# A graph layer with residual and normalisation: near sums kept by feature, gathers paced by TensorE, two rows to a statistic

## The chip, the cores and the metric

One core of one Trainium2 chip. The metric is the device time of one execution in microseconds; lower is better. Times before: 690.98, 693.69 and 698.72 us in three runs, median 693.69 us.

## The reference, cut to what matters

100,000 nodes and 25,000 edges, 128 features, all in fp32. The edges are sorted by `dst`, and `dst` is 100000·u² for a uniform u, so low nodes have many edges and high ones few.

```python
src, tgt = x[row], x[col]                     # 25,000 gathered rows each
h   = relu(concat([src, tgt, edge_attr]) @ W1 + b1)      # 384 -> 128
msg = h @ W2 + b2
w   = sigmoid(concat([msg, conf]) @ Wa + ba)
out = segment_sum(msg * w, col, num_segments=100000)
y   = layernorm(x + out)                      # over the 128 features, eps 1e-5
```

Every node's row is read, normalised and written, also those without an edge.

## The kernel before, in words

**Two ways for edges.** The first 64 tiles of 128 edges (16 groups of `G` = 4 tiles, "near") end at nodes below 91·128 = 11,648. Their sums are gathered in the tile `near`, which holds the x rows of all 91 blocks of 128 nodes. The other 33 groups ("list") lie as runs of 44 edges on each partition; VectorE folds each run edge by edge into `acc`, adds the gathered destination row (`rows_dst`), and the result (`stash`) is normalised and scattered to `out` by an indirect transfer. All nodes from 11,648 on are also read in 63 chunks of 11 rows a partition (`nodes`, six slots), normalised as they are, and written; the scatters come later over those rows.

**Steps.** `STEPS` (line 50) orders the 49 groups, k = 0 to 48: list groups, with a near group after every two, the near groups from high nodes to low. In step k TensorE does `hidden(k)`, the sums of step k-1, `turn(k+1)` (transposes of the gathered rows, their edge attributes, and for near groups a matmul of loaded x rows with the one-hot `pick` in place of a gather) and `messages(k)`. ScalarE copies the turned rows out of PSUM, applies relu, the gate and most of the normalisation. VectorE adds the bias (`raw`, `logit`), folds or adds sums, computes row statistics with `bn_stats`, and normalises the rest. A statistics batch b has three chunks, the list groups of its two steps and, for the nine batches of `NEAR_OUT`, some near blocks; `scales` (L1137) turns its statistics into scale and shift with 13 small instructions and two last ones.

**Near sums.** For each of four tiles of a near group TensorE multiplies the one-hot `place` (edges by nodes, `KA` blocks wide) with `gated` block by block (L921): 192 block matmuls in all, each two passes (the ×384 of a profile). The result has nodes on partitions, and VectorE adds it to a window of `near` that starts at a whole block (L1313, two PSUM banks in turn). The block numbers are read from `block_row` by one load each (L1302). Statistics of near rows are taken directly (L1212).

**GpSimd's queue** is written out in lines 668 to 689: for k = 2 to 48 gather the source rows (four indirect transfers of 128 rows, L641), for list groups also the destination rows (L652), then the scatters that `SCATTERS` names for that k (L662, four transfers a group; 44 transfers stand last, after the gather of k = 48). A gather waits until TensorE has taken the source rows of step k-4 (`RING` = 4, L637). In every second group `pause` (L624) makes GpSimd wait until the group before has landed.

**SyncE's queue** (L552 to L577) issues in each step the attributes, near tables and x rows, chunk loads and chunk stores, each behind its own wait.

Of the kernel before, what the change touches and what calls it, by code (L numbers as in the profile page):

```python
# [8 lines left out]
I32 = mybir.dt.int32  # L9
AX_X = mybir.AxisListType.X  # L10

P = 128
# [3 lines left out]
RING = 4  # L16
SLOTS = 6
PAUSE = 2
TRIO = 3
ROWS = 11  # L20
STATS = 6
# [19 lines left out]
KA = (1, 2, 2, 2, 2, 3, 3, 3, 3, 3, 4, 4, 4, 4, 4, 4)  # L41
LOW = 48
# [22 lines left out]
NEAR_OUT = {4: (77, 91), 5: (70, 77), 13: (59, 70), 14: (48, 59), 15: (37, 48), 19: (26, 37),  # L65
            20: (14, 26), 23: (4, 14), 25: (0, 4)}
NEAR_BATCHES = tuple(sorted(NEAR_OUT))
BATCHES = 26
# [8 lines left out]
SSTEPS = 13  # L77
# [20 lines left out]
def half_of(n, widths):  # L98

    return 8 * (n % 2) if widths[DG - 1 - n] <= 2 else 0  # L100


def before_in_buffer(n, widths):

    alone = n == 0 or widths[DG - 1 - n] > 2 or widths[DG - n] > 2
    return n if alone else n - 1

def sum_uses():  # L110
    uses = []
    for k in range(K + 1):
# [4 lines left out]
        for l in range(LISTS):  # L117
            if k == TAIL_STEP.get(l):
                uses.append(("tail", l))
            if k == HEAD_STEP[l]:  # L120
                uses.append(("head", l))
    return {u: i for i, u in enumerate(uses)}
# [4 lines left out]
EXTRAS = [u for u in USES if u[0] != D_]  # L127
# [6 lines left out]

def columns(b):

    at, n = {}, 0
    if 3 * b < 63:
        at["nodes"] = n
        n += TRIO * ROWS  # L140
# [3 lines left out]
    if b in NEAR_OUT:  # L144
        at["near"] = n
        n += NEAR_OUT[b][1] - NEAR_OUT[b][0]
# [8 lines left out]
NEAR_IN = {0: (76, 91), 1: (62, 76), 2: (48, 62), 6: (32, 48), 8: (16, 32), 10: (0, 16)}  # L155
NEAR_PIECES = 3
ADDED_BEFORE = {4: 2, 5: 2, 13: 6, 14: 6, 15: 6, 19: 10, 20: 10, 23: 13, 25: 16}
# [10 lines left out]
def build(nc, x, src, dstw, attr, conf, W1, b1, W2, b2, Wa, ba, out):  # L168
# [9 lines left out]
    with ExitStack() as ctx:  # L178
# [36 lines left out]
        v_match = sb("v_match", [1, P])  # L215
        base_row = sb("base_row", [1, DT], I32)
        block_row = sb("block_row", [1, DT + 1], I32)
# [13 lines left out]
        raw = sb("raw", [P, 2, G, F])  # L231
# [6 lines left out]
        near = sb("near", [P, NB, F])  # L238
        nodes = sb("nodes", [P, SLOTS, ROWS, F])
        stats = sb("stats", [P, 2, WIDEST, STATS])  # L240
        sc_calc = sb("sc_calc", [P, 5, WIDEST])
        sc = sb("sc", [P, 2, 2, WIDEST])


# [23 lines left out]
        limit = at(4080, 4 * (DT + 1)).rearrange("p (k t) -> p k t", k=4)  # L268
        calc = at(4352, 6 * (DT + 1)).rearrange("p (k t) -> p k t", k=6)
        whole = at(4864, DT + 1, I32)  # L270
# [3 lines left out]
        v_off = at(5400, 4)  # L274
# [27 lines left out]
        g_stats = at(2440, STATS)  # L302
        g_calc = at(2450, 5).rearrange("p (k u) -> p k u", u=1)
# [48 lines left out]
        near_landed = sems("near_landed", 2)  # L352
# [22 lines left out]
        act_normed = sems("act_normed", SLOTS)  # L375
        dve_normed = sems("dve_normed", SLOTS)
        near_act_normed = sem("near_act_normed")
        near_dve_normed = sem("near_dve_normed")
# [6 lines left out]
        v_added = sem("v_added")  # L385

# [28 lines left out]
        def wait(eng, semaphore, value):  # L415
            if value > 0:
                eng.wait_ge(semaphore, value)

# [37 lines left out]
        def _(sp):  # L456
# [49 lines left out]
            def load_near_x(n):  # L506
                g = DG - 1 - n
                at_ = half_of(n, KG)
                done = before_in_buffer(n, KG)
# [4 lines left out]
                for j in range(G):  # L514
                    base = sp.value_load(base_row[0:1, g * G + j:g * G + j + 1], min_val=0, max_val=N - 4 * P)
# [4 lines left out]
            def store_nodes(c):  # L520
                u, nth = c % SLOTS, c // SLOTS + 1
                n = chunk_parts(c)
                sp.wait_ge(act_normed[u], nth)
                sp.wait_ge(dve_normed[u], nth)
# [6 lines left out]
            def store_near(b):  # L531
                q = NEAR_BATCHES.index(b)
                low, high = NEAR_OUT[b]
                sp.wait_ge(near_act_normed, q + 1)
                sp.wait_ge(near_dve_normed, q + 1)
                sp.dma_start(blocks_of(out, low, high), near[:, low:high, :]).then_inc(near_stored[q], 16)
# [966 lines left out]
```

## Time and profile before

| | |
|---|---|
| median of 3 runs | 693.69 us |
| the profiled execution, span | 792.5 us |
| VectorE busy | 502.9 us (63%) |
| GpSimd busy | 457.6 us (58%) |
| ScalarE busy | 427.9 us (54%) |
| TensorE busy | 425.7 us (54%) |
| mean granted TensorE clock | 0.772 |
| DMA | 159.37 MB, mean 201 GB/s |

The profiled execution took some 99 us more than the median of the runs. The page counts only the time in which an engine works; register loads, waits and the gaps between GpSimd's instructions are not in it. "remote" or "another core" is what the profile writes where it cannot name who ended a wait; there is only one core here.

### The profile page before, as it was taken

What the parts mean: (1) busy time and instruction counts of PE and PEld (TensorE: products, weight loads), DVE (VectorE), ACT (ScalarE), POOL (GpSimd) and SP (SyncE); (2) the same over time, 40 slices, a digit from 0 to 9 for tenths busy, and PEclk for the clock granted to TensorE, in tenths of its full rate; (3) what the DMA queues carried; (4) which work ended last, traced back from release to release, by engine and by line L of the source; (5) the groups of instructions that cost most, each with busy time, mean ns of one, the idle gap of its engine ahead of it and who ended that gap; (6) DMA issues with size and microseconds to landing.
All of it is one profiled execution on the core that took longest, in us unless ns stands there. A gap on an engine that the chain in (4) does not pass through costs nothing. (4 is left out here: it accounts for less than half of the span.)

```text
span 792.5 us, 8991 instructions
## 1 busy us (share of the span) xinstructions
PE 425.7 (54%) x1902; PEld 299.8 (38%) x1902; DVE 502.9 (63%) x2146; ACT 427.9 (54%) x1089; POOL 457.6 (58%) x473
## 2 busy tenths in 40 slices
PE   1842778463764136763646566656463475543560
PEld 0531545332543123643435254444251254322250
DVE  5944988878793228883667579888461995330542
ACT  0433686678963047691546567757641698520360
POOL 7676572665666756464755735575746366467330
PEclk9985988777786558985887767977866889776785
DMA  7946678888886226685576568886754657431120
GB/s 190 357 133 208 224 273 299 279 293 254 268 305 207 84 82 219 241 297 171 173 241 199 184 221 264 291 281 232 253 160 133 234 159 233 117 116 59 35 59 14
DMA packets 79882, 159.37 MB, mean 201 GB/s; under 512 B 13970, under 2 KB 48086, under 8 KB 79826
## 3 DMA queue, kind: packets, MB, share of 16 engines
q1 hardware_dynamic: 65106, 129.47, 48.8%
q0 software_dynamic: 14720, 29.32, 13.1%
q8 instruction: 15, 0.25, 0.1%
q14 instruction: 41, 0.34, 0.1%
HBM read 99.75 MB, written 59.95 MB: 202 GB/s over the span
## 5 line engine op out<-in xcount | busy, mean ns | idle before, releaser
L887 PE MATMUL hid_ps<-turned,w 128*128 128x512 f32 x294 | 184.1, 776 | 102.4 <-issue 52.8
L741 ACT ACTIVATE turned<-turn_ps 128x512 f32<-128x512 f32 x147 | 80.3, 590 | 193.5 <-remote 130.0
L760 ACT ACTIVATE nodes<-nodes,sc 128x128 f32<-128x128 f32 (+1 forms) x462 | 184.0, 485 | 0.0
L641 POOL DMA_INDIRECT rows_src<-x,src_list x132 | 131.8, 998 | 85.4 <-issue 36.9
L662 POOL DMA_INDIRECT out<-stash,row_idx x132 | 131.3, 994 | 75.8 <-issue 40.2
L652 POOL DMA_INDIRECT rows_dst<-x,dst_list x132 | 125.8, 953 | 82.8 <-issue 36.2
L1186 DVE BATCH_NORM_STATS2 stats<-nodes 128x6 f32<-128x128 f32 (+1 forms) x693 | 152.8, 278 | 7.7 <-DMA nodes<-x 5.7
L887 PEld LDWEIGHTS hid_ps<-turned,w 128*128 128x128 f32 x294 | 69.6, 253 | 179.7 <-issue 126.5
L921 PE MATMUL sum_ps<-gated,place 128*128 128x128 f32 x384 | 69.1, 342 | 113.6 <-DVE near L1313 62.2
L897 PE MATMUL msg_ps<-w2x,hid 128*128 128x129 f32 x392 | 69.1, 331 | 108.0 <-ACT hid L746 71.4
L921 PEld LDWEIGHTS sum_ps<-gated,place 128*128 128x128 f32 x384 | 60.7, 241 | 131.5 <-DVE near L1313 65.8
L641 POOL DMA_INDIRECT rows_src<-x,src_near x64 | 66.7, 1043 | 67.1 <-PE turn_ps L861 43.8
L897 PEld LDWEIGHTS msg_ps<-w2x,hid 128*128 128x128 f32 x392 | 61.0, 237 | 114.8 <-ACT hid L746 76.0
L1313 DVE TENSOR_TENSOR near<-near,sum_ps 128x512 f32 (+3 forms) x64 | 35.2, 550 | 104.4 <-remote 65.8
L756 ACT ACTIVATE gated<-raw,weight 128x128 f32<-128x128 f32 x196 | 62.6, 390 | 15.4 <-DVE raw L1352 9.9
L1349 DVE TENSOR_TENSOR logit<-msg_ps,lin 128x4 f32<-128x4 f32 x49 | 7.7, 157 | 99.0 <-remote 92.3
L1196 DVE TENSOR_SCALAR nodes<-nodes,sc 128x128 f32<-128x128 f32 (+1 forms) x231 | 68.2, 357 | 0.1
L760 ACT ACTIVATE stash<-stash,sc 128x128 f32<-128x128 f32 x132 | 53.9, 479 | 0.0
L1269 DVE SCALAR_TENSOR_TENSOR acc<-acc,keep,gated 128x128 f32<-128x128 f32 x129 | 43.3, 335 | 15.3 <-remote 7.8
L746 ACT ACTIVATE hid<-hid_ps,b_col 128x512 f32<-128x512 f32 x49 | 32.9, 671 | 36.8 <-remote 21.8
L750 ACT ACTIVATE weight<-logit 128x4 f32<-128x4 f32 x49 | 9.9, 203 | 75.9 <-DVE logit L1349 47.1
L875 PE MATMUL turn_ps<-pick,near_x 128*128 128x128 f32 x280 | 37.9, 295 | 4.9 <-DMA near_x<-x 2.1
(146 smaller groups left out, 510.1 us busy)
## 6 DMA issues: line engine op xcount, KB each, us to landing
nodes<-x SPq DMA_DIRECT2D x62, 704.0 KB
out<-nodes SPq DMA_DIRECT2D x62, 704.0 KB
attr_in<-edge_attr SPq DMA_DIRECT2D x49, 256.0 KB
near_dst<-line SPq DMA_DIRECT2D x16, 256.0 KB
near_x<-x SPq DMA_DIRECT2D x20, 192.0 KB
near_x<-x SPq DMA_DIRECT2D x24, 128.0 KB
out<-near SPq DMA_DIRECT2D x4, 704.0 KB
rows_src<-x,src_list POOLq DMA_INDIRECT x132
```

Source lines behind the costliest of these rows:

```text
L641: pool.indirect_dma_start(out=rows_src[:, k % RING, j, :], out_offset=None, in_=x[:, :], in_offset=bass.IndirectOffsetOnAxis(ap=idx[:, j:j ...
L652: pool.indirect_dma_start(out=rows_dst[:, i % RING, j, :], out_offset=None, in_=x[:, :], in_offset=bass.IndirectOffsetOnAxis(ap=column(dst ...
L662: pool.indirect_dma_start(out=out[:, :], out_offset=bass.IndirectOffsetOnAxis(ap=column(row_idx, i, j), axis=0), in_=stash[:, list_slot(i) ...
L741: act.activation(turned[:, k % 2, c], turn_ps[:, c], ACT.Copy).then_inc(turned_ready, 1)
L756: act.activation(gated[:, k % 2, j, :], raw[:, k % 2, j, :], ACT.Copy, scale=weight[:, k % 2, j:j + 1]).then_inc(gated_ready, 1)
L760: return act.activation(row, row, ACT.Identity, scale=sc[0:parts, b % 2, 0, col:col + 1], bias=sc[0:parts, b % 2, 1, col:col + 1])
L887: last = pe.matmul(hid_ps[:], w1[:, c, :], turned[:, k % 2, c, :], start=(c == 0), stop=(c == 2))
L897: last = pe.matmul(msg(j), hid[:, k % 2, j * P:(j + 1) * P], w2x[:], start=True, stop=True)
L921: last = pe.matmul(sum_ps[:, use % 2, w * P:(w + 1) * P], place[:, b * P:(b + 1) * P], gated[:, k % 2, j, :], start=True, stop=True)
L1186: ins = dve.bn_stats(stats[0:n, b % 2, COLS[b]["nodes"] + i * ROWS + r, :], nodes[0:n, u, r, :])
L1196: ins = dve.tensor_scalar(nodes[0:n, u, r, :], nodes[0:n, u, r, :], sc[0:n, b % 2, 0, col:col + 1], sc[0:n, b % 2, 1, col:col + 1], ALU.mu ...
L1269: dve.scalar_tensor_tensor(acc[:, a, j, :], prev_acc, column(keep, i, j), gated[:, k % 2, j, :], ALU.mult, ALU.add).then_inc(acc_ready, 1)
```

## The change

Four edits in one.

1. **Near sums by feature.** One matmul a tile: `gated` is the weight, `place` the moving side, up to four blocks wide, and the result has features on partitions and nodes in the free direction. `near` holds the sums first, zeroed by two memsets, and VectorE adds at the exact node, so the windows are those of the x rows (`KG` blocks in place of `KA`: 140 blocks in place of 192). When a batch of near rows is final, TensorE transposes its 91 blocks back in 25 pieces of at most four (`turn_sums`), and VectorE adds them to the x rows (`add_rows`), which are loaded now, 14 blocks further up in the same tile. Five of the nine near batches come one or two batches later, as in the new `NEAR_OUT`.
2. **GpSimd.** `pause` is gone. A gather waits until TensorE has done all three turns of step k-2 (`AHEAD` = 2).
3. **Statistics.** `bn_stats` keeps count, mean and squared deviation of even and of odd elements apart. It is now fed two rows element by element in turn, so one instruction gives both rows' statistics: 472 instructions in place of 916 (358, 66 and 48 for chunks, lists and near rows). `scales` has nine small instructions in place of 13.
4. **Tables.** Fewer small instructions before the loop; four block numbers by one load; one semaphore where ScalarE and VectorE each had one; the gate works in place (`gated` for `raw`).

```diff
+AHEAD = 2
-PAUSE = 2
-STATS = 6
+STATS = 3
-NEAR_OUT = {4: (77, 91), 5: (70, 77), 13: (59, 70), 14: (48, 59), 15: (37, 48), 19: (26, 37),
-            20: (14, 26), 23: (4, 14), 25: (0, 4)}
+NEAR_OUT = {5: (77, 91), 7: (70, 77), 13: (59, 70), 15: (48, 59), 17: (37, 48), 19: (26, 37),
+            21: (14, 26), 23: (4, 14), 25: (0, 4)}
-NEAR_IN = {0: (76, 91), 1: (62, 76), 2: (48, 62), 6: (32, 48), 8: (16, 32), 10: (0, 16)}
+NEAR_IN = {0: 5, 11: 7, 15: 13, 27: 15, 31: 17, 35: 19, 39: 21, 43: 23, 44: 25}
...
+def row_pieces(b):
+    low, high = NEAR_OUT[b]
+    pieces = [(b, first, min(first + 4, high)) for first in range(low, high, 4)]
+    if b == BATCHES - 1:
+        return {K: pieces}
+    soon = 2 if ADDED_BEFORE[b] <= 10 else 0
+    return {2 * b - 1: pieces[:soon], 2 * b: pieces[soon:]}
...
             def load_near(k):
                 if k not in NEAR_IN:
                     return
-                low, high = NEAR_IN[k]
-                sp.dma_start(near[:, low:high, :], blocks_of(x, low, high)).then_inc(near_landed[low < LOW], 16)
+                low, high = NEAR_OUT[NEAR_IN[k]]
+                wait(sp, rows_added, taken_before(low + BEHIND, high + BEHIND))
+                sp.dma_start(rows_of(low, high), blocks_of(x, low, high)).then_inc(near_landed, 16)
...
-            def pause(j):
-                landed, value, behind = latest
-                if j == behind and groups[0] % PAUSE == PAUSE - 1:
-                    pool.wait_ge(landed, value)
...
             def gather_src(k):
                 kind, i = STEPS[k]
-                if k >= RING:
-                    pool.wait_ge(turned_ps_ready, 3 * (k - RING) + 1)
+                if k >= AHEAD:
+                    pool.wait_ge(turned_ps_ready, 3 * (k - AHEAD) + 3)
                 idx = table(src_list, i) if kind == S_ else src_near[:, i * G:(i + 1) * G]
                 for j in range(G):
-                    pause(j)
...
             def sum_near(k):
...
-                    for w in range(width):
-                        b = first + j * width + w
-                        last = pe.matmul(sum_ps[:, use % 2, w * P:(w + 1) * P], place[:, b * P:(b + 1) * P],
-                                         gated[:, k % 2, j, :], start=True, stop=True)
-                    last.then_inc(sum_ready, 1)
+                    b = first + j * width
+                    pe.matmul(sum_ps[:, use % 2, 0:width * P], gated[:, k % 2, j, :], place[:, b * P:(b + width) * P],
+                              start=True, stop=True).then_inc(sum_ready, 1)
+
+            def turn_sums(b, low, high):
+                use = USE[("rows", b, low, high)]
+                bank_free(use)
+                pe.wait_ge(near_added, G * ADDED_BEFORE[b])
+                pe.wait_ge(v_added, 1)
+                for i in range(low, high):
+                    last = pe.transpose(sum_ps[:, use % 2, (i - low) * P:(i - low + 1) * P], near[:, i * P:(i + 1) * P],
+                                        ident[:])
+                last.then_inc(sum_ready, 1)
...
+            step(dve.memset(near[:, 0:NB // 2 * F], 0.0))
...
             def scales(st, calc_, to, sem_, base, final, beside=()):
-                mean_e, m2_e, mean_o, m2_o = (st[:, :, i] for i in (1, 2, 4, 5))
+                mean, m2 = st[:, :, 1], st[:, :, 2]
-                then(dve.tensor_tensor(mean2, mean_e, mean_o, ALU.add), False)
-                then(dve.tensor_tensor(apart, mean_e, mean_o, ALU.subtract), False)
-                then(dve.tensor_tensor(v, m2_e, m2_o, ALU.add))
-                then(dve.scalar_tensor_tensor(a, apart, F / 4.0, apart, ALU.mult, ALU.mult))
-                then(dve.scalar_tensor_tensor(v, v, F * EPS, a, ALU.add, ALU.add))
+                then(dve.tensor_scalar(v, m2, F * EPS, None, ALU.add))
...
+            def pair_stats(st, rows):
+                pair = rows.rearrange("p w f -> p f w")
+                if rows.shape[1] == 1:
+                    pair = pair.to_broadcast([rows.shape[0], F, 2])
+                return dve.bn_stats(st.rearrange("p w k -> p (w k)"), pair)
...
             def sum_near(k, beside):
-                blocks = [dve.value_load(block_row[0:1, g * G + j:g * G + j + 1], min_val=0, max_val=NB - width)
-                          for j in range(G)]
+                bases = loaded(dve.engine, base_row[0:1, g * G:(g + 1) * G], (NB - width) * P)
...
+            def add_rows(b, low, high):
+                use = USE[("rows", b, low, high)]
+                dve.wait_ge(near_landed, 16 * (NEAR_BATCHES.index(b) + 1))
+                dve.wait_ge(sum_ready, use + 1)
+                rows_ = rows_of(low, high)
+                dve.tensor_tensor(rows_, rows_, sum_ps[:, use % 2, 0:(high - low) * P].rearrange("p (b f) -> p b f", f=F),
+                                  ALU.add).then_inc(rows_added, 1)
+
+            step(dve.memset(near[:, NB // 2 * F:NB * F], 0.0))
             settle()
```

## Rows read from the trace of the kernel before

**Rows 1.** The page: the span, and busy us (share of span) xinstructions of each engine.
```profile
span 792.5 us, 8991 instructions
DVE  5944988878793228883667579888461995330542
POOL 7676572665666756464755735575746366467330
```

**Rows 2.** The page, costliest groups: the indirect transfers that GpSimd issues.
```profile
L641 POOL DMA_INDIRECT rows_src<-x,src_list x132 | 131.8, 998 | 85.4 <-issue 36.9
L662 POOL DMA_INDIRECT out<-stash,row_idx x132 | 131.3, 994 | 75.8 <-issue 40.2
L652 POOL DMA_INDIRECT rows_dst<-x,dst_list x132 | 125.8, 953 | 82.8 <-issue 36.2
L641 POOL DMA_INDIRECT rows_src<-x,src_near x64 | 66.7, 1043 | 67.1 <-PE turn_ps L861 43.8
```

**Rows 3.** Who GpSimd waited for: us in total, times, longest us.
```profile
POOL rows_src L641 <- PE turn_ps L861: 68.7, 11, 11.0
POOL rows_dst L652 <- DVE stash L1288: 31.7, 7, 14.5
POOL rows_dst L652 <- DMA rows_src<-x,src_list: 12.5, 6, 2.6
POOL out L662 <- DMA out<-stash,row_idx: 10.7, 4, 3.9
POOL rows_src L641 <- DMA rows_dst<-x,dst_list: 7.9, 4, 3.2
```

**Rows 4.** Timeline, 258 to 289 us: start us, us, instruction [idle before <-releaser].
```profile
258.49 1.06 PE L880 MATMUL turn_ps<-ident,attr_in 128*128 128x128 f32 x4
267.55 0.60 ACT L741 ACTIVATE turned<-turn_ps 128x512 f32<-128x512 f32 x1 [22.20 <-remote]
277.33 0.60 ACT L741 ACTIVATE turned<-turn_ps 128x512 f32<-128x512 f32 x1 [9.19 <-remote]
288.53 0.60 ACT L741 ACTIVATE turned<-turn_ps 128x512 f32<-128x512 f32 x1 [10.60 <-remote]
```

**Rows 5.** ScalarE's longest wait by total: us in total, times, longest us.
```profile
ACT turned L741 <- remote: 130.0, 23, 23.9
```

**Rows 6.** Busy us (xinstructions) by engine in two stretches; then clock, DMA share, GB/s.
```profile
260.00:280.00 20.00, 0.63 (x6) 0.44 (x4) 4.33 (x21) 1.20 (x2) 14.89 (x17) 0.58 0.20 52
480.00:500.00 20.00, 16.99 (x70) 11.76 (x70) 18.79 (x84) 17.56 (x46) 12.78 (x14) 0.79 0.79 243
```

**Rows 7.** Timeline of VectorE: fourteen statistics of one row each, back to back.
```profile
486.30 2.79 DVE L1186 BATCH_NORM_STATS2 stats<-nodes 128x6 f32<-128x128 f32 x14
```

**Rows 8.** Groups by form: a spaced read (L1151) and a dense one (L1157).
```profile
L1151 DVE TENSOR_TENSOR sc_calc<-stats 128x48 f32<-128x48 f32 x4 | 1.0, 246 | 0.6 <-DVE stats L1212 0.5
L1157 DVE TENSOR_TENSOR sc_calc<-sc_calc 128x48 f32<-128x48 f32 x4 | 0.8, 208 | 0.3 <-DVE sc_calc L1156 0.3
L1151 DVE TENSOR_TENSOR sc_calc<-stats 128x4 f32<-128x4 f32 x2 | 0.3, 162 | 0.0
L1157 DVE TENSOR_TENSOR sc_calc<-sc_calc 128x4 f32<-128x4 f32 x2 | 0.3, 162 | 0.0
```

**Rows 9.** By form: near adds of four blocks and one; near sums on TensorE.
```profile
L1313 DVE TENSOR_TENSOR near<-near,sum_ps 128x512 f32 x24 | 16.4, 683 | 41.0 <-remote 20.4 <-PE sum_ps L921 12.5 <-issue 8.0
L1313 DVE TENSOR_TENSOR near<-near,sum_ps 128x128 f32 x4 | 1.1, 287 | 4.1 <-issue 3.2 <-PE sum_ps L921 0.7 <-DVE near L1313 0.2
L921 PE MATMUL sum_ps<-gated,place 128*128 128x128 f32 x384 | 69.1, 342 | 113.6 <-DVE near L1313 62.2 <-ACT gated L756 31.1 <-issue 20.3
```

**Rows 10.** Loads of block numbers (L1302) on VectorE's queue: duration ns min/median/max.
```profile
L1302 DVEq TENSOR_LOAD <-block_row x64: 296/304/1387, 81.7 to 771.8; - x64
```

**Rows 11.** Timeline of GpSimd: gather 48 starts; its last scatter, at the end.
```profile
688.23 0.96 POOL L641 DMA_INDIRECT rows_src<-x,src_near  x1 [7.70 <-PE turn_ps L861]
...
768.57 0.97 POOL L662 DMA_INDIRECT out<-stash,row_idx  x1 [0.30 <-issue]
```

More of the change, by code:

```diff
@@ L121, in sum_uses @@
                 uses.append(("head", l))
+        uses += [("rows", *p) for p in row_pieces_at(k)]
     return {u: i for i, u in enumerate(uses)}
@@ L126, with taken_before, even, crosses @@
 USES = list(USE)
-EXTRAS = [u for u in USES if u[0] != D_]
+EXTRAS = [u for u in USES if u[0] not in (D_, "rows")]
+PIECES = [u[1:] for u in USES if u[0] == "rows"]
+def taken_before(first, last):
+    return max((i + 1 for i, (_, low, high) in enumerate(PIECES) if low < last and high > first), default=0)
 def list_groups_of(b):
     return [STEPS[k - 1][1] for k in (2 * b - 1, 2 * b) if is_list(k - 1)]
+def even(n):
+    return n + n % 2
+def crosses(b):
+    return 3 * b + 2 < 62
+def node_column(b, i, r):
+    before = 0 if i == 0 else even(ROWS) + (i - 1) * (ROWS if crosses(b) else even(ROWS))
+    return COLS[b]["nodes"] + before + r
 def columns(b):
@@ L145, in columns @@
         at["near"] = n
[L146 removed]
+        n += even(NEAR_OUT[b][1] - NEAR_OUT[b][0])
     return at, n
@@ L417, in wait, with loaded @@
                 eng.wait_ge(semaphore, value)
+        def loaded(engine, row, most):
+            _, values = nc.values_load_multi_w_load_instructions(
+                row, engines=(engine,), min_val=0, max_val=most,
+                skip_runtime_bounds_check_because="VectorE holds the row between its bounds when it makes it")
+            return values
         def chunk_parts(c):
@@ L906, in bank_free @@
                     pe.wait_ge(near_added, G * which[0] + which[1] + 1)
+                elif kind == "rows":
+                    pe.wait_ge(rows_added, PIECES.index(tuple(which)) + 1)
                 else:
@@ L1100, in _ @@
             settle()
-            step(dve.tensor_reduce(flags[0:1, 0:1], c[4], AX_X, ALU.add))
+            step(dve.tensor_reduce(flags[0:1, 0:1], c[1], AX_X, ALU.add))
             dve.wait_ge(consts_in, 16 * 8)
@@ L1198, in norm_row @@
                 if r == ROWS - 1:
-                    ins.then_inc(dve_normed[u], 1)
+                    ins.then_inc(normed[u], 1)
             def list_stats(i, b):
                 dve.wait_ge(stashed, i + 1)
-                for j in range(G):
-                    last = dve.bn_stats(stats[:, b % 2, COLS[b][i] + j, :], stash[:, list_slot(i) + j, :])
+                for j in range(0, G, 2):
+                    w, row = COLS[b][i] + j, list_slot(i) + j
+                    last = pair_stats(stats[:, b % 2, w:w + 2, :], stash[:, row:row + 2, :])
                 last.then_inc(stat_ready, 1)
@@ L1395, in _ @@
                     add_v()
+                for piece in row_pieces_at(k):
+                    add_rows(*piece)
                 if is_near(k):
```

241 lines of the change are left out of this document (106 added, 135 removed).

## The prediction, made before the changed kernel was run

> **What bounds the kernel now.** I read the page's busy shares first. No engine is full: VectorE works 502.9 us of 792.5, GpSimd 457.6 [rows 1]. GpSimd's figure hides something, though. It issues 460 indirect transfers, 0.95 to 1.04 us each in the mean of the four groups [rows 2], and between two of them lie 0.30 us even where nothing is waited for, as before its last scatter [rows 11]. With the gap one costs 1.27 to 1.28 us (0.97 + 0.30), and 460 of them some 587 us. That is the floor of any version with these transfers, plus the head and the tail. Second, GpSimd's waits: 68.7 us in 11 waits for TensorE at L641, 31.7 us for VectorE, and waits for landings, which are the pauses: the three largest make 12.5 + 10.7 + 7.9 = 31.1 us in 14 waits [rows 3]. So GpSimd sets the pace, or is close to it, and the others must keep up.
>
> Third, the timeline of a bad stretch. TensorE finishes the third turn at 259.55 us (258.49 + 1.06), yet ScalarE copies the three turned tiles at 267.55, 277.33 and 288.53 us, each time behind a wait whose end the profile cannot name [rows 4]. Such waits of ScalarE make 130.0 us in 23 pieces, the longest 23.9 us [rows 5]. In this stretch VectorE works 4.33 us of 20 and ScalarE 1.20, while GpSimd works 14.89, without a rest; in a good stretch VectorE works 18.79 of 20 and GpSimd 12.78 [rows 6]. The reader is to see two things. TensorE's signals arrive late while GpSimd issues without a break, here 29 us for three signals. And in good stretches VectorE is the full engine (94%), so its work counts there.
>
> The profiled execution has a span of 792.5 us, the median of the runs is 693.69. The missing 99 us are most likely such held signals, which the unprofiled runs would then have less of. My sum is made on the rows of the profiled execution; since its terms are differences, I take them over to the median, and cut the one term that consists of holds.
>
> **GpSimd: the pauses go.** At most their 31.1 us, at least nothing, if GpSimd then waits at the next gate. GpSimd is the pacing engine, so I take all: -31.
>
> **GpSimd: the gate moves** from the first turn of step k-4 to the third of k-2. Between two gates stand at most 4 + 4 gathers and 8 scatters, 16 transfers, 20.4 us. A hold like the one of 29.0 us would end after 20.4 us, 30% earlier, because GpSimd would stand still. 30% of 130.0 us is -39; the median run holds less than the profiled one, so I take -33, with bounds of 0 and -99 (all that divides the two times). The gate can also cost: that is a rival below. Queued behind a waiting gather are the destination gathers and scatters of the same step; the scatters free `stash` slots 14 groups later, so nobody waits for them soon. The rule that speaks against this term comes from the Trainium skill, page SBUF — State Buffer, section Who interferes with whom: TensorE and ScalarE never wait on anyone. By it GpSimd's streaks would not touch TensorE, the term would be 0 and the sum 33 higher (the lower end of rival C). The trace does not agree: ScalarE stood 23.9 us behind work that TensorE had finished [rows 5].
>
> **Statistics in pairs.** 916 instructions of one row become 472 of two. Fourteen in a row take 2.79 us, 0.199 us each [rows 7], so 916 are 182 us. How long does a pair take? An element costs 1.05 ns where the read is dense ((208 - 162)/44) and 1.91 ns where neighbours lie 24 bytes apart ((246 - 162)/44), both from 4 and 48 elements a partition [rows 8]. One row is 128 x 1.05 = 134 ns and a fixed 65. A pair has 256 elements, which lie 512 bytes apart in turn: dense it would cost 0.334 us, and 472 of them 158 (-25 us); spaced 0.554 us, 261 (+79 us). The nearest row is the spaced one, so I take +79, with -25 as the other end. The Trainium skill has rules on both sides. Advanced Engine Details and Errata, section SBUF Cachelines, says that a read which changes its 16-byte line with each element pays; the 1.91 ns agree, for 24 bytes. VectorE: DVE Perf Modes, section Rules for kernel authors, says to keep the number of instructions low; by that alone the pairs gain.
>
> **The rest of VectorE.** Four of 13 small instructions go in 25 batches, 0.16 to 0.25 us each [rows 8], two of them overlapped: 100 x 0.14 = -14. Near adds: 0.683 us for four blocks, 0.287 for one, so 0.132 a block and 0.155 fixed [rows 9]; 52 blocks fewer are -7. `place` shrinks by the same 52 blocks, between 0 and -7, say -3. Of 64 loads of 0.304 us [rows 10] three in four go, 14.6 us, partly behind `pick`: -10. `add_rows` is new: 25 x 0.155 + 91 x 0.132 = +16. Together with the pairs +61 us, or -43 with dense reads. VectorE is full in the good stretches only and busy 63% over all, so half comes through: +30 (or -22). The gate in place and the shared semaphores cost nothing.
>
> **TensorE.** 384 passes take 69.1 us, 0.180 each [rows 9]. 140 blocks in place of 192 save 19, 91 transposes of one pass each cost 16: nothing. The 25 pieces are also 25 more handovers through the two banks of `sum_ps`; the first two of a batch are made while VectorE folds a list group, and only later ones wait. I count them as covered; uncovered they would cost one add each, 25 x 0.68 = 17 us.
>
> **SyncE.** Nine loads of near rows now stand behind a wait for pieces that are due a step before, ahead of chunk stores. The six slots of chunks cover it: nothing; if not, a step (693.69/49 = 14 us) for each that is late.
>
> **Head and tail.** The first memset lies in VectorE's wait for the first table. The second, of 46 x 128 elements a partition, stands ahead of the first statistics: at 1.05 ns an element 6 us, at nothing 0; some dozen small table instructions go in exchange: +2. At the end gather 48 starts at 688.23 us and the last scatter ends at 769.54 [rows 11]: 81 us for 48 transfers that need 61, so 20 us of waits, and 23 us to the end of the span. The new gate lets gather 48 go two steps later, 2 x 14 = 28 us. The waits absorb most of it, but all 44 scatters now lie beside the last two steps and hold their signals. Between 0 and +28: +10.
>
> **Sum.** -31 - 33 + 30 + 10 + 2 = -22: 693.69 - 22 = 672, so 671 to 672 us.
>
> **Rivals.**
> *B, pairs at dense speed.* For it: the second row of a pair may stay at hand in another way than the 24-byte read shows, and no row has two streams in turn. Against it: rows 8. It gives 672 - 52 = 620 us. Chance 0.20.
> *C, the gates cost more than the pauses: slower.* GpSimd is at the floor of 587 us only if it never waits, and a lead of two steps leaves it little. Each of its waits for TensorE lasts 6.2 us now (68.7/11) [rows 3]. If 16 of 47 gates wait so long, that is 99 us in place of 68.7, +30. If the streaks of 16 transfers hold TensorE's signals just as before, the 33 us do not come: 672 + 30 + 33 = 735 us; with the 33 alone it is 705. It decides from the point where GpSimd's waits for TensorE at its source gathers pass 91 us (68.7 + 22), 1.9 us a gate. For it: rows 4, since a gate that needs a later signal waits for a held one. Against it: then GpSimd stands still and lets the signals through. Chance 0.27.
> *D, nothing to measure.* The gates take back the pauses' 31 us and half of VectorE's extra work (15 us) finds room there: 672 + 31 - 15 = 688 us, which with small deviations is no change. Chance 0.14.
> *A, the forecast*, has 0.39.
>
> **Numbers.** A's own range is 650 to 690. The range to be given takes in C's lower half and B's upper half: 622 to 724, and leaves out about 0.09 below and 0.11 above. A measurement of this kernel tells about 1% (7 us) from no change. Faster by more than that: A nearly whole and B, 0.57. Within: 0.14. Slower: 0.29.
>
> **What would show it.** In the changed profile: no waits of GpSimd for landings of transfers that stand two back, and no streak of more than 16 transfers in the loop; ScalarE's unnamed waits at L741 below 100 us; a pair's mean near 0.6 us rather than 0.4, and VectorE's busy time near 560 us; if it is near 460, B holds. GpSimd's waits for TensorE above 91 us show C. The forecast fails if those waits rise as much as the pauses fall, or if the last 44 scatters end more than 28 us later against TensorE's last turn.

## The result, and the profile after

| | kernel before | changed kernel |
|---|---|---|
| median, us | 695.53 (690.98 to 698.72, 4 runs) | 633.04 (631.06 to 636.57, 4 runs) |
| ratio | | 0.9099 (95%: 0.9048 to 0.9151) |
| profiled execution, span | 792.5 [rows 1] | 631.2 |

The change takes 62 us off. The forecast was 22 us off, 671 us. The direction was right and the time lies inside the range of 622 to 724, but the gain is almost three times the one forecast, so terms of the sum were badly sized. What follows finds the main one: it is the first, the pauses of GpSimd.

The page of the changed kernel: busy us of each engine, then two lines of busy tenths in 40 slices. (In [rows 1] the two engine lines are such tenths too; the busy us of before stand in the table of the section on time and profile before.)

```profile
span 631.2 us, 7693 instructions
PE 394.6 (63%) x1737; PEld 265.1 (42%) x1737; DVE 472.7 (75%) x1561; ACT 425.2 (67%) x1089; POOL 457.5 (72%) x473
DVE  6899998989895888849688869989779759274200
POOL 7575577777477777777777777777777777777772
```

GpSimd is as busy as before, 457.5 us, but now evenly so: its line is nearly all sevens, because one transfer takes about 0.97 us and the gap behind it 0.30. Before, the line has sixes, fives and fours all along. The page's costliest groups of GpSimd, against [rows 2] (busy, mean ns of one, idle before them):

```profile
L689 POOL DMA_INDIRECT out<-stash,row_idx x132 | 135.0, 1023 | 47.3 <-issue 39.3
L672 POOL DMA_INDIRECT rows_src<-x,src_list x132 | 131.1, 993 | 51.3 <-issue 38.7
L681 POOL DMA_INDIRECT rows_dst<-x,dst_list x132 | 127.7, 968 | 40.2 <-issue 39.9
L672 POOL DMA_INDIRECT rows_src<-x,src_near x64 | 61.7, 965 | 22.3 <-issue 18.9
```

The durations are nearly the old ones; the idle time of the three groups of 132 has gone from 75 to 85 us each to 40 to 51. Who GpSimd still waited for, against [rows 3] (us in total, times, longest):

```profile
POOL rows_src L672 <- issue: 57.6, 189, 0.3
POOL rows_dst L681 <- issue: 39.9, 131, 0.3
POOL out L689 <- issue: 39.3, 129, 0.3
POOL rows_src L672 <- PE turn_ps L907: 15.1, 4, 9.3
POOL out L689 <- DMA out<-near: 7.4, 1, 7.4
```

449 gaps of 0.3 us make 136.8 us; true waits make 22.5. The first transfer begins at 3.2 us and the last ends at 619.5. In between, GpSimd issues 192 transfers (373.0 to 619.5 us) without any wait, and not one wait of ScalarE in the whole profile is "remote", the word that stood 23 times in [rows 5]:

```profile
ACT turned L767 <- PE turn_ps L888: 48.0, 15, 5.7
ACT turned L767 <- PE turn_ps L893: 37.3, 13, 5.2
```

VectorE by groups, then a stretch of its timeline (start us, us), against [rows 7, 9]:

```profile
L1186 DVE BATCH_NORM_STATS2 stats<-nodes 128x6 f32<-128x256 f32 (+1 forms) x358 | 133.6, 418 | 7.0 <-DMA nodes<-x 6.9
L1186 DVE BATCH_NORM_STATS2 stats<-stash 128x6 f32<-128x256 f32 x66 | 25.2, 423 | 1.5
L1186 DVE BATCH_NORM_STATS2 stats<-near 128x6 f32<-128x256 f32 x48 | 16.7, 416 | 0.2
L1343 DVE TENSOR_TENSOR near<-near,sum_ps 128x256 f32 (+3 forms) x64 | 28.0, 437 | 28.9 <-PE sum_ps L949 28.1 <-DVE near L1343 0.8
L1400 DVE TENSOR_TENSOR near<-near,sum_ps 128x512 f32<-128x512 f32 (+2 forms) x25 | 15.0, 628 | 1.5 <-PE sum_ps L959 1.5
L1403 DVE MEMSET near<- 128x5888 f32 x1 | 5.0, 4965 | 1.2 <-issue 1.2
```

```profile
489.83 1.42 DVE L1186 BATCH_NORM_STATS2 stats<-nodes 128x6 f32<-128x256 f32 x4
```

Four pairs take 1.42 us back to back, 0.355 each. The forecast had 0.334 for a dense read and 0.554 for a spaced one, and took the spaced one. All 472 pairs have 175.5 us of busy time.

### The profile page after: what moved, and what is told of

The parts are those of the page before. It is cut to its first block and busy times, and to the rows that moved or that the text cites. A ratio compares the mean times of both kernels' runs of the same rounds, so it can differ in the third digit from the quotient of the medians.

```text
span 631.2 us, 7693 instructions
## 1 busy us (share of the span) xinstructions
PE 394.6 (63%) x1737; PEld 265.1 (42%) x1737; DVE 472.7 (75%) x1561; ACT 425.2 (67%) x1089; POOL 457.5 (72%) x473
## 5 line engine op out<-in xcount | busy, mean ns | idle before, releaser
L914 PE MATMUL hid_ps<-turned,w 128*128 128x512 f32 x294 | 162.8, 697 | 4.1 <-ACT turned L767 4.0
L1186 DVE BATCH_NORM_STATS2 stats<-nodes 128x6 f32<-128x256 f32 (+1 forms) x358 | 133.6, 418 | 7.0 <-DMA nodes<-x 6.9
L914 PEld LDWEIGHTS hid_ps<-turned,w 128*128 128x128 f32 x294 | 63.7, 233 | 69.0 <-issue 61.2
L672 POOL DMA_INDIRECT rows_src<-x,src_near x64 | 61.7, 965 | 22.3 <-issue 18.9
L782 ACT ACTIVATE gated<-gated,weight 128x128 f32<-128x128 f32 x196 | 62.6, 390 | 9.9 <-DVE gated L1381 6.7
L893 PE MATMUL turn_ps<-ident,rows_dst 128*128 128x128 f32 x132 | 27.1, 342 | 56.5 <-DMA rows_dst<-x,dst_list 56.5
L888 PE MATMUL turn_ps<-ident,rows_src 128*128 128x128 f32 x196 | 33.4, 298 | 37.7 <-DMA rows_src<-x,src_list 37.2
L949 PE MATMUL sum_ps<-place,gated 128*128 128x256 f32 (+3 forms) x128 | 44.0, 454 | 14.3 <-ACT gated L782 9.9
L1343 DVE TENSOR_TENSOR near<-near,sum_ps 128x256 f32 (+3 forms) x64 | 28.0, 437 | 28.9 <-PE sum_ps L949 28.1
L888 PEld LDWEIGHTS turn_ps<-ident,rows_src 128*128 128x128 f32 x196 | 25.3, 153 | 54.4 <-DMA rows_src<-x,src_list 44.2
L893 PEld LDWEIGHTS turn_ps<-ident,rows_dst 128*128 128x128 f32 x132 | 18.9, 173 | 61.3 <-DMA rows_dst<-x,dst_list 61.3
```

Source lines behind the costliest of these rows:

```text
L672: pool.indirect_dma_start(out=rows_src[:, k % RING, j, :], out_offset=None, in_=x[:, :], in_offset=bass.IndirectOffsetOnAxis(ap=idx[:, j:j ...
L782: act.activation(gated[:, k % 2, j, :], gated[:, k % 2, j, :], ACT.Copy, scale=weight[:, k % 2, j:j + 1]).then_inc(gated_ready, 1)
L888: last = pe.transpose(turn_ps[:, 0, j * P:(j + 1) * P], rows_src[:, s, j, :], ident[:])
L893: last = pe.transpose(turn_ps[:, 1, j * P:(j + 1) * P], rows_dst[:, i % RING, j, :], ident[:])
L914: last = pe.matmul(hid_ps[:], w1[:, c, :], turned[:, k % 2, c, :], start=(c == 0), stop=(c == 2))
L1186: return dve.bn_stats(st.rearrange("p w k -> p (w k)"), pair)
```

## The experiments

There were sixteen runs of thirteen kernels, in four calls; the runs of one call stand on one chip, beside runs of the kernel before. One thing must be known to read them: in the first call the kernel before took 814.68 us (7 runs), in the other three 694.48, 692.04 and 692.42. Where it takes 815 us, the profile has the late signals of [rows 4, 5], where it takes 693 it has none. So numbers are compared inside a call, or it is said that they stand in two.

### First call: the two queue edits alone, where signals come late

*b_same*, the kernel before, unchanged, for its profile.

> The kernel before, unchanged, as the scale for the others and for a second profile. Theory H (TensorE's signals are held by something that belongs to the kernel before): the profile shows unnamed waits of ScalarE at the turned rows again, 100 us or more in total, and a span well above the median. Rival N (the first profile was an outlier): span within 10 us of the timed median of about 695 us, unnamed waits below 30 us. Timed: 693 to 698 us under both.

*b_nopause*, the kernel before without pauses:

```diff
             def pause(j):
                 landed, value, behind = latest
-                if j == behind and groups[0] % PAUSE == PAUSE - 1:
-                    pool.wait_ge(landed, value)
+                return
```

> The kernel before without its pauses, the gate at step k-4 kept. Theory P (the pauses are the bound: GpSimd is at its floor of 587 us and each pause delays it): 650 to 665 us, GpSimd issues in streaks of dozens, its busy time unchanged. Rival G (what matters is how far GpSimd may run ahead, not the pauses): 690 to 700 us, and the held signals stay or grow. The prediction had 31 us for the pauses, so 664 us.

*b_gate2*, the kernel before with the new gate, pauses kept:

```diff
-                if k >= RING:
-                    pool.wait_ge(turned_ps_ready, 3 * (k - RING) + 1)
+                if k >= 2:
+                    pool.wait_ge(turned_ps_ready, 3 * (k - 2) + 3)
```

> The kernel before with the new gate (all three turns of step k-2), pauses kept. Theory P: 685 to 705 us, nothing gained, since the pauses stay. Rival G: 655 to 670 us and no held signals; the prediction had 33 us for this part alone.

*b_queue*, both edits.

> The kernel before with both edits of GpSimd's queue: no pauses and the gate at k-2. Prediction's sum: 694 - 31 - 33 + 10 = 640 us. Theory P: the same as without pauses alone, within 5 us. Rival V (VectorE's work and the near sums carry the gain of 62 us, the queue little): above 680 us.

| | median, us | ratio (95%) |
|---|---|---|
| b_same | 815.56 | |
| b_nopause | 839.86 | 1.0302 (1.0185 to 1.0419) |
| b_gate2 | 778.00 | 0.9579 (0.9491 to 0.9666) |
| b_queue | 802.36 | 0.984 (0.9724 to 0.9955) |

The three results count as unclear, though none of their intervals takes in 1. As far as they go, the prediction's picture of late signals holds for the gate, where the nearer one makes the kernel faster; its term for the pauses has the wrong sign here. The expectations missed: the kernel before was to take 693 to 698 us, and neither theory had 839.86 us without pauses or 778.00 with the nearer gate. Waits in the profile of b_same (us, times, longest):

```profile
ACT turned L741 <- remote: 131.8, 20, 25.5
POOL rows_src L641 <- PE turn_ps L861: 65.4, 9, 17.0
POOL rows_dst L652 <- DMA rows_src<-x,src_list: 13.3, 6, 2.7
POOL out L662 <- DMA out<-stash,row_idx: 8.6, 3, 3.8
```

They are those of [rows 3, 5] almost to the number, and its span is 807.5 us: the profile on which the prediction was made was one of this condition, while the runs it was to forecast were not. In the profile of b_nopause:

```profile
POOL rows_src L640 <- PE turn_ps L860: 122.5, 17, 11.2
POOL rows_dst L651 <- DVE stash L1287: 55.6, 9, 16.0
POOL out L661 <- ACT stash L759: 25.6, 5, 15.7
```

The gates and the stash take back more than the pauses gave: what GpSimd no longer waits for landings (42.9 us in 17 waits in b_same) it waits for the others. In b_gate2 ScalarE's remote waits at the turned rows fall to 70.5 us in 25. None of this can explain a gain of 9%: with both edits the kernel gains 1.6%. Something else worked in the 633 us.

### Second call: the changed kernel with parts taken back

*a_same*, the changed kernel, unchanged.

> The changed kernel, unchanged, as the scale for the others. The kernel before took 815 us on the chip of the first four runs and 695 us on the first chip, so the held signals of TensorE belong to a chip or its state, not to the kernel alone. Theory Q (the changed kernel gives TensorE's signals room on any chip): on a chip where before takes over 780 us this takes 640 to 680 us. Rival R (a chip that holds signals holds them here too): 720 to 780 us there. On a chip where before takes about 695 us both say 633 us.

*a_gate4*, the changed kernel with the old gate:

```diff
-                if k >= AHEAD:
-                    pool.wait_ge(turned_ps_ready, 3 * (k - AHEAD) + 3)
+                if k >= RING:
+                    pool.wait_ge(turned_ps_ready, 3 * (k - RING) + 1)
```

> The changed kernel with the old gate (first turn of step k-4). The profile of the changed kernel has 15.1 us of waits at the gate and one streak of 192 transfers, so where signals are not held the gate hardly closes: within 1% of the changed kernel, or up to 10 us faster, since the gather starts earlier (theory F: GpSimd is at its floor). Where signals are held, the gate at k-2 gained 37 us (4.2%) in the kernel before, so this would be 3 to 5% slower than the changed kernel (theory G).

*a_pause*, the changed kernel with the pauses back:

```diff
+            def pause(j):
+                landed, value, behind = latest
+                if j == behind and groups[0] % 2 == 1:
+                    pool.wait_ge(landed, value)
...
                 for j in range(G):
+                    pause(j)
...
+                group_begun(src_got[k % RING], 16 * G * (k // RING + 1), 2)
```

> The changed kernel with the pauses put back, the new gate kept. Theory F (GpSimd paces the changed kernel, 460 transfers of 1.28 us): each pause adds its wait, 25 to 50 us, so 5 to 8% slower. Rival V (VectorE or TensorE pace it): within 1%. Where signals are held, the kernel before without pauses was 3% slower than with them, so pauses would help: up to 3% faster there.

*a_oldqueue*, both taken back.

> The changed kernel with GpSimd's whole old queue (pauses, gate at k-4). What is left against the kernel before is then the near sums by feature, the pairs and the tables. Theory F: these alone gain little where GpSimd paces, so 4 to 8% over the changed kernel. Rival V: within 1.5% of the changed kernel, since VectorE's saved work carries the gain.

| | median, us | ratio (95%) | span of the profile | GpSimd's waits for landings |
|---|---|---|---|---|
| a_same | 631.44 | 0.9107 (0.9054 to 0.9159) | 629.1 | |
| a_gate4 | 632.68 | 0.9098 (0.9048 to 0.9148) | 631.5 | |
| a_pause | 700.25 | 1.0089 (1.005 to 1.0129) | 698.5 | 93.2 us in 40 |
| a_oldqueue | 698.15 | 1.0063 (1.0027 to 1.0099) | 693.1 | 93.3 us in 39 |

(The last column counts the waits for the landing of an indirect transfer.) This settles which part it is in the changed kernel. The pauses alone cost 69 us (700.25 - 631.44), more than the whole gain and more than the 25 to 50 us expected of them. The rest of the change, the new sums, the pairs and the gate, together gains nothing as long as the pauses stand: a_pause is at 1.0089, if anything slower than the kernel before. The waits of a_pause show what a pause costs here:

```profile
POOL rows_dst L696 <- DMA rows_src<-x,src_list: 27.2, 12, 3.5
POOL out L706 <- DMA out<-stash,row_idx: 23.4, 9, 4.8
POOL rows_src L685 <- DMA out<-stash,row_idx: 19.0, 6, 4.7
```

### Third call: the same edits on the kernel before, where signals come in time

*b_nopause_2* is b_nopause again.

> The kernel before without its pauses, gate at k-4, again. In the changed kernel the pauses cost 69 us (631 to 700) where signals are not held. Theory F (the pauses are the whole gain, since GpSimd is at its floor): 630 to 645 us on a chip where before takes about 695. Rival V (the gain also needs VectorE's lighter work): 650 to 680 us. Where before takes about 815 us: 840 us again.

*b_queue_2* is b_queue again.

> The kernel before with both queue edits, again. Where signals are not held, theory F: 630 to 645 us, within 1% of the kernel without pauses alone, since in the changed kernel the gate made no difference (632.7 against 631.4 us). Rival V: 650 to 680 us. Where before takes about 815 us: 802 us again.

*b_queue_pairs* is b_queue with the statistics in pairs, and with them the nine small instructions of `scales` in place of 13 (the diff is cut to the pairs):

```diff
...
+            def pair_stats(st, rows):
+                pair = rows.rearrange("p w f -> p f w")
+                if rows.shape[1] == 1:
+                    pair = pair.to_broadcast([rows.shape[0], F, 2])
+                return dve.bn_stats(st.rearrange("p w k -> p (w k)"), pair)
...
```

> The kernel before with both queue edits and statistics in pairs; near sums and tables stay old. Against the queue edits alone: theory F: within 1% (VectorE's work is beside GpSimd's). Rival V: 15 to 25 us faster, as dense pairs save VectorE about 25 + 14 us of busy time. VectorE's busy time should fall from about 503 to 465 us under both.

*a_scatter3* is the changed kernel with three of four scatters:

```diff
-                for j in range(G):
+                for j in range(G - 1):
...
-                pool.wait_ge(scattered[g], 16 * G * len(range(g, LISTS * LG, STASH_G)))
+                pool.wait_ge(scattered[g], 16 * (G - 1) * len(range(g, LISTS * LG, STASH_G)))
```

> The changed kernel with three of four scatter transfers in each list group (a quarter of the list rows is not written to the output): 33 of 460 indirect transfers fewer, 33 x 1.28 = 42 us less of GpSimd's queue. Theory F (GpSimd paces): 631 - 42 = 589 us, at least 30 us of it. Rival V (VectorE, 473 us busy, and the loop through TensorE are as near to the bound): less than 15 us gained.

| | median, us | ratio (95%) | VectorE busy, us |
|---|---|---|---|
| b_nopause_2 | 628.72 | 0.9084 (0.9007 to 0.9161) | 499.8 |
| b_queue_2 | 640.80 | 0.9274 (0.9201 to 0.9346) | 499.6 |
| b_queue_pairs | 630.67 | 0.9103 (0.9041 to 0.9165) | 462.0 |
| a_scatter3 | 595.66 | 0.8599 (0.8539 to 0.8659) | 471.7 |

b_nopause_2 is the key run. Leaving out the pauses in the kernel before gives 63 us (692.04 - 628.72), all that the whole change gives: 0.9084 against 0.9099, so near sums, pairs, tables and gate together add nothing that can be told from it. (Three of its executions took 628.37 to 629.04 us and one took 871.25; the median of the three alone is 628.39.) The nearer gate then costs 12 us (640.80 - 628.72), where less than 1% was expected. GpSimd's waits at it, b_queue_2:

```profile
POOL rows_src L639 <- PE turn_ps L878: 27.9, 9, 13.7
```

The pairs give 10 us behind that gate (640.80 - 630.67): VectorE loses 37.6 us of work, and GpSimd's waits at the gate fall from 27.9 us to 17.0. That is more than the 1% of theory F and less than the 15 us of rival V. In a_scatter3, 33 transfers fewer give 36 us (631.44 - 595.66, over two calls) where 33 x 1.27 = 42 were possible, with VectorE's work unchanged at 471.7. GpSimd's queue is the bound of the changed kernel; a_scatter3 waits 18.4 us at the gate, where the changed kernel had 15.1.

### Fourth call: the quiet profile of before, the dose, and a better version

Open was why pauses that showed 31 to 48 us of waits [rows 3] cost 63 to 69, and whether the other parts are worth anything without the gate.

*b_same_2* is the kernel before again, for a profile where signals come in time.

> The kernel before, unchanged, for its profile where TensorE's signals are not held. Theory W (the profile that the prediction was read from hid the pauses: GpSimd stood at its gates there, and what it had issued landed meanwhile): the waits for landings sum to 80 to 100 us in about 40 waits here, where that profile had 48 us in 21; span about 693 us; no waits for TensorE at the source gathers. Rival: again about 48 us, and the rest of the 66 us that the pauses cost lies elsewhere.

*a_pause4* is a_pause with a pause in every fourth group instead of every second:

```diff
-                if j == behind and groups[0] % 2 == 1:
+                if j == behind and groups[0] % 4 == 3:
```

> The changed kernel with a pause in every fourth group in place of every second (which took 700 us). Theory F (each pause adds its own wait to a queue that is at its floor): half of the cost, 631 + 35 = 666 us, within 8 us. Rival (something else in the waiting group costs, such as transfers that land in another order): 631 to 645 or above 685 us.

*b_nopause_pairs* is b_nopause with the pairs.

> The kernel before without pauses and with statistics in pairs; gate, near sums and tables old. It is the candidate for a version that beats both: without pauses alone 628.7 us, the pairs took 10 us off where the gate at k-2 was in. Theory F: the gate hardly closes at k-4, VectorE's work is hidden, 625 to 629 us. Rival V (the pairs' 10 us come on top): 618 to 622 us.

*a_gate4_late* is the changed kernel with the old gate, and the first two scatter groups one step later:

```diff
-SCATTERS = {15: (0, 1), 18: (2, 3),
+SCATTERS = {16: (0, 1), 18: (2, 3),
```

> The changed kernel with the gate at k-4 and the first two list groups scattered one step later (k = 16 in place of 15). With the gate at k-4 alone GpSimd waited 13.7 us for the store of the first near rows ahead of the first scatter, and 8.0 us for VectorE. Theory F: the wait for the store shrinks by the 10 us of one step's gathers, 620 to 627 us. Rival: another wait takes its place, 630 to 634 us.

| | median, us | ratio (95%) | span of the profile |
|---|---|---|---|
| b_same_2 | 698.81 (1 run) | | 697.0 |
| a_pause4 | 664.49 | 0.9517 (0.9445 to 0.9589) | 664.2 |
| b_nopause_pairs | 625.47 | 0.9031 (0.8989 to 0.9073) | 624.1 |
| a_gate4_late | 621.59 | 0.897 (0.8933 to 0.9007) | 624.9 |

The page of b_same_2, and who its GpSimd waited for:

```profile
span 697.0 us, 8991 instructions
PE 402.7 (58%) x1902; PEld 289.8 (42%) x1902; DVE 499.9 (72%) x2146; ACT 427.7 (61%) x1089; POOL 458.1 (66%) x473
```

```profile
POOL rows_dst L652 <- DMA rows_src<-x,src_list: 38.8, 14, 4.8
POOL out L662 <- DMA out<-stash,row_idx: 24.3, 10, 5.9
POOL rows_src L641 <- DMA out<-stash,row_idx: 16.4, 5, 4.8
POOL rows_src L641 <- DMA rows_dst<-x,dst_list: 5.9, 2, 3.1
POOL out L662 <- DMA rows_src<-x,src_near: 5.2, 4, 1.7
POOL rows_src L641 <- DMA rows_src<-x,src_near: 3.2, 1, 3.2
POOL rows_dst L652 <- DMA rows_dst<-x,dst_list: 2.6, 1, 2.6
POOL rows_src L641 <- DMA rows_src<-x,src_list: 1.0, 1, 1.0
POOL rows_src L641 <- PE turn_ps L861: 0.3, 1, 0.3
```

The same kernel as in [rows 3], and another picture. Landings: 97.4 us in 38 waits (the eight lines that name an indirect transfer as releaser), not 48.5 in 21. Gates: 0.3 us, not 68.7. The queue has 57 pauses, each in the middle of a group: two transfers of the new group (one behind a scatter group) go first, then the group before must have landed. In the profile of before 14 of the 57 come behind a wait of 1.5 to 14.5 us in their own group, and just one of these 14 waits again, 1.4 us. The other 43 also wait less than here, 1.1 us each against 1.5 (beyond the ordinary gap); why is not shown. The same view of b_nopause_2:

```profile
POOL rows_src L640 <- issue: 57.3, 188, 0.3
POOL out L661 <- issue: 40.2, 132, 0.3
POOL rows_dst L651 <- issue: 38.7, 127, 0.3
POOL rows_dst L651 <- DVE stash L1287: 17.1, 4, 10.3
```

Now the difference can be accounted for. The landing waits fall by 97.4. Of them the ordinary gap of 0.3 us stays (the gaps "issue" rise from 127.4 to 136.2, +8.8), and the stash takes 16.8 (17.1 - 0.3). 97.4 - 8.8 - 16.8 = 71.8, and the spans differ by 70.4 (697.0 - 626.6, over two calls; the profiled execution of b_same_2 is a long one, 698.81 us against a median of 692.42, so 63 us remain between the medians). The dose agrees: in a_pause4 the landings make 46.6 us in 19 waits, half of a_pause's 93.2 in 40, and the time lies 33 us above a_same, half of 69 (over two calls).

A gain of the pairs without the near gate is small, if there is one: b_nopause_pairs lies 3 us under b_nopause_2 (over two calls), and the intervals of the two ratios overlap. Last, a_gate4_late beats both kernels: 621.59 us, and its interval, 0.8933 to 0.9007, lies wholly below that of a_same, 0.9054 to 0.9159. Its waits:

```profile
POOL out L688 <- DMA out<-near: 5.7, 1, 5.7
POOL rows_dst L680 <- DVE stash L1322: 5.9, 2, 4.6
```

In a_gate4 these two lines were 13.7 and 8.0 us. The first scatter of all must wait until `near` has been written out, and behind it stand the gathers of the next steps; one step later it waits 5.7. Where the two edits are not taken apart the share of each is open; a_gate4 says that the gate alone gives nothing.

## Why the prediction was wrong in size, point by point

**What bounds the kernel: right.** A GpSimd that never waits needs 1.27 us a transfer, which gives the forecast's floor of 587 us, plus head and tail. The changed kernel does 460 transfers in 616 us with 22.5 us of waits, and a_scatter3 shows that transfers taken out come out of the time.

**"GpSimd: the pauses go", -31: the step that failed.** It measured -63 (b_nopause_2 against the kernel before) and +69 when put back (a_pause). The mechanism, a pacing engine that gets its waits back, was the one named; the size was read from an execution that was not of the kind forecast. In it GpSimd stood 68.7 us at the gates behind late signals, and a pause behind such a stand finds that the group before has landed (14 of 57 pauses, of which one waits). That explains part of the low figure; the other 43 pauses waited less too, for a reason that no run shows. In an execution where the signals come in time the gates cost 0.3 us and the pauses 97.4. Two things in view could have warned. The profiled span was 99 us above the median, which the text noted, and then used for another term only. And the text took just the three largest lines and called them the most that the pauses could give, where all waits for landings made 48.5 us.

**"GpSimd: the gate moves", -33: wrong for these runs.** It was the term made of late signals. Where they occur, the nearer gate gives 37 us (b_gate2, 814.68 to 778.00), close to the -33. Where they don't, it gives nothing to the changed kernel (631.44 against 632.68) and costs the kernel before 12 us (b_queue_2). Its explanation was wrong for these runs also: streaks of GpSimd were to hold TensorE's signals, and were to be 16 transfers long at most. Yet 192 transfers in a row in the changed kernel, and 352 in b_nopause_2, hold none. There the sentence of the Trainium skill that the prediction set aside (SBUF — State Buffer, Who interferes with whom) agrees with the traces. It does not say what holds the signals in the other condition, and the traces leave it open. In b_same ScalarE's waits of 12.6 and 25.5 us end 3.1 and 4.1 us after GpSimd had come to a stop, but one of 22.3 us ends in the middle of a streak of 26. The size of the holds was also read too large. The prediction has ScalarE stand 23.9 us "behind work that TensorE had finished"; a wait in [rows 4, 5] counts from ScalarE's own last instruction. TensorE's first turn of the stretch of [rows 4] ran here:

```profile
256.79 1.06 PE L861 MATMUL turn_ps<-ident,rows_src 128*128 128x128 f32 x4
```

Of the 22.2 us that ScalarE waited for it until 267.55, only 9.7 lie behind its end at 257.85. Of the wait of 23.9 us it is 12.7 (TensorE's turn ended at 726.37, the copy began at 739.11). So the 130.0 us, of which the term took 30%, were not all holds. The two errors offset each other, which was luck: -33 that did not come, and -32 that the pauses gave above their 31.

**"Statistics in pairs", +79: wrong, it was the other end.** Busy time of the statistics went from 200.5 us (153.3 + 28.8 + 18.4 in b_same_2) to 175.5, that is -25.0, the dense end. By the forecast's own reckoning, back to back, it is less: 472 x 0.355 = 168 us against 182, or -15; either way near the dense end and far from +79. The nearest row for a spaced read was a two-input add of 48 elements at 24 bytes (1.91 ns an element); one `bn_stats` over two rows 512 bytes apart pays (355 - 65)/256 = 1.13 ns, if its fixed part is the 65 ns estimated for one row. The rule quoted from the Trainium skill (Advanced Engine Details and Errata, SBUF Cachelines) therefore did not hold for this instruction, or the lines of both rows stay at hand; no run tells these apart. The Trainium skill's other rule (VectorE: DVE Perf Modes, Rules for kernel authors) agrees in sign with -25.

**"The rest of VectorE": sizes right, effect absent.** Near adds 35.1 to 28.0 (-7.1, forecast -7); `place` 23.3 to 19.5 (-3.8, forecast -3); `add_rows` 15.0 (forecast 16). VectorE's busy time fell 27.2 us (499.9 to 472.7), and half of such a sum was to come through. It did not: beside a queue that paces, 37 us less work on VectorE gave 3 us (b_nopause_pairs) and, behind the near gate, 10. So the +30 for all of VectorE was wrong twice, in its sign and in what comes through.

**TensorE and SyncE at nothing: not contradicted.** b_queue_pairs and a_same differ by all of the near sums, the turning back and the block tables, and stand at 0.9103 (0.9041 to 0.9165) and 0.9107 (0.9054 to 0.9159). The 25 new handovers cost VectorE 1.5 us of waiting for `sum_ps`. One cost had no term: the first near batch is final one batch later, and the first scatter waits for its store, 7.4 us in the changed kernel and 13.7 in a_gate4, where b_nopause_2 has no such wait above the ordinary gap.

**Head and tail, +2 and +10.** The second memset took 5.0 us (forecast 6). GpSimd's first and last of the 44 closing scatters, in the profile after, against [rows 11]:

```profile
563.55 1.01 POOL L689 DMA_INDIRECT out<-stash,row_idx  x1 [0.30 <-issue]
...
618.57 0.97 POOL L689 DMA_INDIRECT out<-stash,row_idx  x1 [0.30 <-issue]
```

They take 56 us (619.54 - 563.55) without a wait, and the span ends 11.7 us behind them; the last 48 transfers take 61 us. The prediction read 81 us for them and 23 us to the end from [rows 11]. Of the 20 us of waits in there 19.1 were waits for ScalarE's `stash`, in three pieces; b_same_2, where signals come in time, has none of them. There the kernel before starts its last 48 transfers with the first line and ends them with the last:

```profile
623.40 0.95 POOL L641 DMA_INDIRECT rows_src<-x,src_near  x1 [0.30 <-issue]
...
684.38 0.97 POOL L662 DMA_INDIRECT out<-stash,row_idx  x1 [0.30 <-issue]
```

That is 62 us, and the end comes 11.7 us later, as in the changed kernel. So the tail neither gained nor lost, and the +10 did not come.

**The sum put right.** -22 as forecast; -32 for the pauses (63 in place of 31); +33 for late signals that these runs don't have; -30 for VectorE, whose work neither grew nor sets the time; -12 for head and tail, of which nothing was seen: -63, where -62 was measured. The -30 and the -12 only take back terms that did not come; neither was measured by itself.

**The rivals.** *B* had the pairs' price right and the reason for a gain wrong: its 620 us came from VectorE, which paces nothing. *C* happened in small: the near gate costs the kernel before 12 us, with 27.9 us of waits at it, where the rival put 91 us as the point from which it decides. *D* did not happen: GpSimd waited 15.1 us at the gates, not the pauses' 31 us more than before. Its result, no change, is met only where the pauses stay (a_pause, 1.0089). Of the signs to look for, two were named rightly: waits of GpSimd for landings are gone, and a pair near 0.4 us with VectorE near 460 was to show the dense read. One was not: no streak was to be longer than 16 transfers.

**Open.** What makes TensorE's signals late in some executions was not found. It was seen in the first call and in the profile of [rows 1 to 11], and a long streak of transfers alone does not bring it about. Whether the execution of b_nopause_2 that took 871.25 us was of that kind is not known: no trace of it was kept, and its granted clock was 1.0, where the runs of the first call had 0.75 to 0.77. The changed kernel never ran in that condition, so whether it would lose there, as b_nopause does (3%), is not known.

## What to carry to other kernels

Price a term in an execution that looks like the runs to be forecast: when the profile's own time lies 14% above the median, its waits belong to another state, and a wait that looks small there may be small because another one stood in front of it. A wait at the engine that paces everything is worth its length less the gap that stays and what the next gate takes; the same microseconds on an engine beside it are worth almost nothing. If the price of an access pattern has no row of its own instruction, keep both ends of the bound open rather than choose one by likeness.

## What the runs showed of the hardware that was not expected

- GpSimd's queue sustains an indirect transfer of 128 rows of 512 bytes every 1.28 us, 192 in a row in the changed kernel (246.5 us), and every 1.30 us, 352 in a row in b_nopause_2 (457.3 us): in the profile after, 0.97 to 1.02 us in the mean of each group and 0.30 between two transfers.
- Waiting for the group before to land, with two transfers issued in between (one behind a scatter group), costs 2.6 us in the mean of the 38 waits of b_same_2 (97.4/38), up to 5.9.
- One program has two regimes (694 and 815 us for the kernel before, 629 and 840 for the one without pauses, in different calls), told in a profile by "remote" releasers: 131.8 us at ScalarE's turned copies in b_same, none in b_same_2. An edit can change sign between them: the pauses' removal is worth -63 us in one and +25 (839.86 - 814.68) in the other.
- `bn_stats` over two rows that lie 512 bytes apart takes 0.355 us for 256 elements, an estimated 1.13 ns an element, against 1.05 for a dense read of an add.
- A memset of 5,888 fp32 elements a partition takes 4.97 us, 0.84 ns an element.
